# Feed-forward stage of a gated attention kernel: two chunks per turn on TensorE, weight splitting moved within the slot, two small buffers allocated first

## What is computed

```python
def block(x, w1, b1, w2, b2):            # the six feed-forward blocks, DIM 256, HIDDEN 1024
    h = gelu(einsum('bsd,hd->bsh', x, w1) + b1)
    return einsum('bsh,dh->bsd', h, w2) + b2 + x

xn = layernorm(x)
s = attention(xn, w_qkv, w_out)          # causal, 16 heads of 16
f = xn
for i in range(6):
    f = block(f, W1[i], B1[i], W2[i], B2[i])
    if i < 5:
        f = layernorm(f) * LN_G[i] + LN_B[i]
out = x + s * silu(f)
```

## Time and profile before

| | |
|---|---|
| median of three runs | 1671.97 us (1671.54 to 1676.83) |
| the profiled execution, its own time | 1672.36 us |
| its span in the trace | 1670.7 us |
| PE busy | 1617.1 us, 97% |
| PEld busy | 1314.5 us, 79% |
| DVE busy | 1169.8 us, 70% |
| ACT busy | 856.2 us, 51% |
| POOL busy | 317.8 us, 19% |
| mean granted clock of TensorE | 0.992 |

### The profile page before, as it was taken

The page is one execution under the profiler, slowest core; times in us unless marked ns, Lnnn a source line. Parts: engine busy times, 40 slices in busy tenths (PEclk is TensorE's granted clock), DMA queues, the critical chain, the costliest instruction groups (busy, mean ns, idle before and its releaser), DMA issues. The chain is left out here.

```text
span 1670.7 us, 28636 instructions
## 1 busy us (share of the span) xinstructions
PE 1617.1 (97%) x11024; PEld 1314.5 (79%) x11024; DVE 1169.8 (70%) x2932; ACT 856.2 (51%) x1164; POOL 317.8 (19%) x305
## 2 busy tenths in 40 slices
PE   6989999999999999999999999999999899999998
PEld 5879988889888888888888888888989844444443
DVE  7826777777777777777777677776565568787753
ACT  3444444444443444444444444444444499798986
POOL 1021111111111111111111111111011123343333
PEclk9989999999999999999999999999999989999999
DMA  8868724536002002012030020022020135565341
GB/s 276 320 173 209 174 62 109 116 73 140 15 7 61 8 16 49 7 34 42 7 51 8 23 51 9 14 39 80 1 71 1 45 114 163 162 187 178 117 116 58
DMA packets 76017, 141.46 MB, mean 85 GB/s; under 512 B 10172, under 2 KB 52924, under 8 KB 68540
## 3 DMA queue, kind: packets, MB, share of 16 engines
q1 hardware_dynamic: 75880, 139.62, 32.0%
HBM read 109.44 MB, written 55.31 MB: 99 GB/s over the span
## 5 line engine op out<-in xcount | busy, mean ns | idle before, releaser
L646 ACT ACTIVATE m_hid<-m_h_ps,m_b1s 128x512 f32<-128x512 f32 x384 | 265.3, 691 | 694.1 <-PE m_h_ps L749 674.6
L712 DVE TENSOR_TENSOR m_hidl<-m_hid,m_hidh 128x512 fp32r<-128x512 f32 x384 | 283.1, 737 | 266.5 <-ACT m_hidh L649 265.6
L993 ACT ACTIVATE a_prob<-a_st_ps 128x1024 f32<-128x1024 f32 x288 | 277.6, 1023 | 40.4 <-PE a_st_ps L1079 36.9
L762 PE MATMUL m_y_ps<-shared,m_hidh 128*128 128x256 f32 x1536 | 283.1, 282 | 0.0
L749 PE MATMUL m_h_ps<-m_xth,shared 128*128 128x512 f32 x768 | 275.7, 400 | 6.3 <-issue 3.9
L613 POOL TENSOR_TENSOR xres<-xres,m_b2s 128x1024 f32<-128x1024 f32 x48 | 132.1, 2753 | 744.1 <-DVE xres L665 744.1
L649 ACT ACTIVATE m_hidh<-m_h_ps,m_b1s 128x512 fp32r<-128x512 f32 x384 | 261.7, 682 | 0.0
L762 PEld LDWEIGHTS m_y_ps<-shared,m_hidh 128*128 128x128 f32 x1536 | 246.8, 188 | 14.5
L762 PE MATMUL m_y_ps<-w2h,m_hidh 128*128 128x256 f32 x768 | 216.9, 282 | 0.0
L762 PE MATMUL m_y_ps<-shared,m_hidl 128*128 128x256 f32 x768 | 215.3, 280 | 0.0
L762 PE MATMUL m_y_ps<-w2l,m_hidh 128*128 128x256 f32 x768 | 214.2, 279 | 0.0
(11 more groups left out here) (121 smaller groups left out, 2656.6 us busy)
## 6 DMA issues: line engine op xcount, KB each, us to landing
shared<-k_stacks SPq DMA_DIRECT2D x14, 896.0 KB
shared<-q_stacks SPq DMA_DIRECT2D x14, 896.0 KB
q_stacks<-q_parts SPq DMA_DIRECT2D x96, 128.0 KB
k_stacks<-k_parts SPq DMA_DIRECT2D x96, 128.0 KB
q_parts<-mq SPq DMA_DIRECT2D x16, 512.0 KB, 4.3
k_parts<-mk SPq DMA_DIRECT2D x16, 512.0 KB, 3.8
mk<-k_stacks SPq DMA_DIRECT2D x20, 384.0 KB, 10.7
raw<-w1t SPq DMA_DIRECT2D x48, 128.0 KB, 2.3
```

Of the source, the lines that this page charges most:

```text
L646: nc.scalar.activation(hid[n % 2][:], h_ps[n % 2][:], ACT.Gelu, bias=b1s[i % 2][:, k:k + 1])
L712: nc.vector.tensor_tensor(hidl[n % 4][:], hid[n % 2][:], hidh[n % 4][:].bitcast(F32), ALU.subtract).then_inc(low_done, 1)
L762: m = nc.tensor.matmul(y_ps[:, j, :], h[n % 4][:, j * P:(j + 1) * P], w[par][:, k, :], start=(k == 0 and j % 2 == 0 and h is hidh and w is ...
L993: nc.scalar.activation(to, scores, ACT.Exp).then_inc(exp_done, 1)
```

## The change

TensorE takes two chunks per turn: `up(n)`, `up(n + 1)`, the transposes where they are due, the visit of chunk `n`, `down(n - 2)`, `down(n - 1)`, the visit of chunk `n + 1`. The visits stand at `k` = 0, 1, 2, 4 and 5 of a slot in place of 1 to 6. On VectorE the steps of the epilogue move: `add_y` from `k = 0` to 1, the statistics from 2 to 4, aggregation and variance from 3 and 4 to 5, scaling from 5 to 6, the last step from 6 to 7. `split_piece` moves from `k = 7` to `k = 2`. The constants `mhalf` and the first maxima buffer `x_mx0` are made before all other buffers.

```diff
-        s.mx = [b.sb(f"x_mx{u}", [P, 2, HG, QT]) for u in range(2)]
+        s.mx = [*mx, b.sb("x_mx1", [P, 2, HG, QT])]
...
+        VISITED = (0, 1, 2, 4, 5)
         AT = {}
         for v in range(VISITS):
-            n = 6 * (SLOTS - FROM) * v // VISITS
-            AT.setdefault(CH * (FROM + n // 6) + 1 + n % 6, []).append(v)
+            n = len(VISITED) * (SLOTS - FROM) * v // VISITS
+            AT.setdefault(CH * (FROM + n // len(VISITED)) + VISITED[n % len(VISITED)], []).append(v)
...
-                if k == 0:
+                if k == 1:
                     add_y(t, 0)
                     add_y(t, 1)
...
-                if k == 2:
+                if k == 4:
                     dve.wait_ge(b2_added, t + 1)
...
-                elif k == 3:
+                elif k == 5:
                     dve.wait_ge(stats_done, t + 1)
...
-                elif k == 4:
                     dve.wait_ge(mean_done, t + 1)
...
-                elif k == 5:
+                elif k == 6:
...
-                elif k == 6:
+                elif k == 7:
...
-                if k == 7 and t < LAST:
+                if k == 2 and t < LAST:
                     dve.wait_ge(raw_loaded[g % 2], 32 * (t // 2 + 1))
                     split_piece(nc, dve, keep, (i + 1) % 2, g, w_high, t + 1).then_inc(w_split, 1)
...
-            for n in range(CHUNKS + 2):
+            for n in range(0, CHUNKS + 2, 2):
                 if n < CHUNKS:
                     up(n)
+                    up(n + 1)
                 if n % CH == 2 and n // CH + 1 < SLOTS:
                     turn(n // CH + 1)
+                for v in AT.get(n, ()):
+                    search.pe_visit(pe, s_ps, v, True)
                 if n >= 2:
                     down(n - 2)
-                for v in AT.get(n, ()):
+                    down(n - 1)
+                for v in AT.get(n + 1, ()):
                     search.pe_visit(pe, s_ps, v, True)
...
+        mhalf = b.sb("mhalf", [P, TILES])
+        mx = [b.sb("x_mx0", [P, 2, HG, QT])]
         apart = [b.sb(f"apart{u}", [P, PAIR * SEQ], F32R) for u in range(2)]
         shared = [b.sb(f"shared{n}", [P, HALVES * HID], F32R) for n in range(4)]
```

More of the change, by code:

```diff
@@ L135, with __init__ @@
 class MaxSearch:
-    def __init__(s, nc, b, scratch, keep):
+    def __init__(s, nc, b, scratch, keep, mx):
         s.nc, s.scratch = nc, scratch
@@ L721, in _ @@
                     search.dve_visit(dve, s_ps, v)
-            epilogue(SLOTS - 1, 0)
+            epilogue(SLOTS - 1, 1)
         @block.tensor
@@ L1152, in gated_block @@
         keep = {
-            "ident": b.sb("ident", [P, P]), "mhalf": b.sb("mhalf", [P, TILES]), "causal": b.sb("causal", [P, BANK]),
+            "ident": b.sb("ident", [P, P]), "mhalf": mhalf, "causal": b.sb("causal", [P, BANK]),
             "ones": b.sb("ones", [SPARE, 1, P]),
@@ L1167, in gated_block @@
         }
-        search = MaxSearch(nc, b, scratch, keep)
+        search = MaxSearch(nc, b, scratch, keep, mx)
         with ExitStack() as inner:
```

## The result

The changed kernel takes 1651.67 us (median of four runs, 1651.39 to 1652.38) against 1672.84 us for the kernel before in the same comparison: 0.987 of its time, with a 95% interval of 0.9852 to 0.9888. The profiled execution's span is 1650.7 us, 20.0 us less than before.

A forecast was written before the change was run, and what follows sets the result against it. TensorE's list was taken to bound stage two, 1236.5 of 1670.7 us. Terms -10.7 (block starts), -1.7 (clock), +15.7 (first split), -10 (visits), -9 (buffers) sum to -15.7 us: 1656.3 us forecast, range 1649 to 1668.

The forecast's parts named there:

- block starts: Five block starts where TensorE waits for the weight split: the split at `k = 2` removes the waits, -10.7 us.
- first split: Slot 0: VectorE waits for `raw` at the early split, TensorE stands 13.4 us before `down(3)`, then half clock; +15.7 us.
- visits: TensorE's nineteen stage-two waits for VectorE's maxima: 9 to 19 us, less 4 at most at `k = 5`; -10 us taken.
- buffers: First weight set moved to the second's addresses up to a multiple of 8192, to match its pace: -9 us, bounds 0 and 10.
- pairs as such: Grouping TensorE's list by two chunks: no gap at either seam between first and second products, so costed at nothing.
- in slot 1 and later `raw` is in time: Slot 1 onward: weight DMAs arrive before the early split needs them, all else being 15.7 us later too.
- rival 3: Visits at `k = 5`: VectorE's chain 0.6 us longer, so 42 visits lose 0.7 us each; 1695 us, slower; chance 0.06.
- The steps of the layer norm: Their moves within the slot on VectorE: result needed eight slots later, so hidden, at nothing.
- Rival 1: First weight set slow for its region or partner operands, so the address term is nothing: 1665.3 us; chance 0.25.
- Rival 2: Address term nothing and visits gain nothing, `k = 5` giving back the rest: 1672 us, no change; chance 0.1 with neighbours.
- Rival 4: Slot 0's pause does not come because the DMAs into `raw` land early: 1640.6 us; chance 0.04.
- slot 40 "nearly as early": Sign in the timeline: slot 3 starts some 15 us later than before, slot 40 nearly as early.

The follow-up runs named there:

- a2: The changed kernel with `mhalf` and `x_mx0` back in their old places: 1662.70 us, 0.9937 of the kernel before.
- b4: The changed kernel with TensorE's list back to one chunk per turn, all other edits kept: 1656.03 us, 0.9903 of the kernel before.
- a1: The changed kernel with the two DMAs of the first weight eighth ahead of the layout work in SyncE's list: 1643.63 us, 0.9826 of the kernel before.
- a7: The changed kernel with two weight pieces fetched ahead of the layout work and the third ahead of slot 1's search loads: 1637.16 us, 0.9789 of the kernel before.
- a3: The changed kernel with the split back at `k = 7`: 1661.17 us, 0.9928 of the kernel before.
- b2: The kernel before with only `split_piece` moved from `k = 7` to `k = 2`: 1687.77 us, 1.0087 of the kernel before.
- b1: The kernel before with only `mhalf` and `x_mx0` made first: 1666.38 us, 0.9957 of the kernel before.
- a4: The changed kernel with only `mhalf` made first, `x_mx0` not: 1653.78 us, 0.9887 of the kernel before.
- a6: a7 with 32 unused bytes per partition ahead of `raw`, the weights staying in place: 1659.44 us, 0.9909 of the kernel before.

## Why the prediction was right

I forecast 1656.3 us, in a range of 1649 to 1668, by a sum of -15.7 us. The time is 1651.67, 21.2 us below the run of before beside it and 20.0 us by the spans. The mechanisms came as told, one of them not where I had put it, and two terms were too small.

| term | forecast, us | measured, us | read from |
|---|---|---|---|
| block starts | -10.7 | -10.3 | 0.11 us at block 3 for 2.18, five times |
| clock at block 4 | -1.7 | -1.7 | no such stretch after |
| first split | +15.7 | +16.2 | slot 1's start, less slot 0's |
| visits | -10 | -11 | waits of 4.5 us gone, distances at the visits |
| buffers | -9 | -9.5 to -11 | a2 |
| pairs as such | 0 | -3.7 to -4.4 | b4 |

The visits' -11 is an estimate, good to some 2 us since a few per cent of the matmuls' rows are missing: the excess of the distances at visits over what a stream has is 13.4 us over the stage before and 5.8 after, of which 3.7 (41 x 0.09 us) is the seam behind transposes, which the kernel before has too, at a second product. The measured terms add up to -20.0 us with the smaller values and -22.2 with the larger, against -20.0 in the spans.

*The first split.* The chain was right step by step: VectorE's wait of 19.0 us (I said some 18), the last ready product at 114.9 (115.0), the subtraction at 128.04 and the pause of 13.6 (13.4), half clock behind it. a1 shows the cause, since with the DMAs early slot 1 starts at 122.41. The step "in slot 1 and later `raw` is in time" held only because the pause itself had given SyncE 16 us; in a1, without it, two later pieces were late. It takes three pieces (a7).

*The block starts.* Gone, as worked out. I did not see what a3 shows: with the layer norm's last step at `k = 7`, ahead of a split left there, the late split would have cost 24 us, so that in this kernel the edit is worth twice the 12 us that it is worth before.

*Visits.* The size was near, the reasoning was not. I counted on pairs giving the maximum both `down` to finish in. b4, without pairs, has no visit waits either; what helps is that visits and VectorE's heavy steps stand at other `k`. In the changed kernel no wait is left at the tight `k = 5`, so rival 3 did not come.

*The steps of the layer norm, "hidden, at nothing".* True of the changed kernel and wrong of the edit: b2 shows that with the steps in their old places the early split loses 12 us more than I had expected of it, and the kernel is slower than before; a3 shows that the last step would lengthen the gap at a late split. This cover was part of the change's gain, and I should have written what the split costs at a chunk that also holds the statistics.

*The grouping, "at nothing".* This is the term of the sum that was furthest off. b4 puts it at 4.4 us. I had looked at the seams, where there is no gap, and not at the first second products behind a seam, which follow each other 3 to 7 ns more slowly than the later ones. The distances account for 2.8 us of it.

*The buffers.* The bound from the earlier trace rows, 9.6 us, was right: a2 gives 9.5 us up to the last second product and 11.0 in the medians. Rival 1 has fallen. Of the two rules of the Trainium skill that I had weighed against this term, the first does not fit these runs. TensorE: Matmul & The Clock Gate, section "Wait — 56ns, not 53.3ns?", gives a distance by column count alone, and here, with the order of a7 and only buffers moved, 512 columns take 230 to 233.5 ns and 256 columns 114.5 to 119.2 ns. SBUF — State Buffer, section "Who interferes with whom", says that TensorE never waits on anyone, which can be so and still leave this, as the same work of the other engines runs beside both rates.

*Rival 2* (visits and addresses nothing) fell with a2. *Rival 4* did not come in the changed kernel, but its price was right to a few us: forecast 1640.6 for a kernel without the pause; a7, which takes the pause out, is 14.5 us below the changed one.

My sign of slot 40 "nearly as early" did not follow from my own sum, by which slot 40 had to be 15 us earlier or nearly so; it is 17.8 us earlier.

**Open.** Why the distance between the starts of two SBUF tiles should set TensorE's pace, and whether the distance modulo 256 or the places of the first set decide it (a first set that is 64 apart at other places would tell). Why second products just behind first ones are slower. b1's missing 4 us: 1.7 us of its profiled execution is the second stretch of half clock and 1.6 us lies at visits, but whether its other executions had that stretch is not known.

## What to carry to other kernels

Before an instruction that waits for a DMA is moved earlier in a hand-written list, read when that DMA is issued and what stands ahead of it in the issuing engine's list; here a few lines that moved three fetches ahead of the layout work gave nearly as much again (14.5 us) as the whole change (21.2 us). Where two tiles of the same kind run at different paces in one kernel, compare their addresses with those of their partner operands, and try a pad of 32 or 64 bytes: here 32 bytes ahead of the first set gained 9 us (a4 against a2), and 32 bytes ahead of `raw` cost 22 (a6 against a7). And an edit that is "hidden" should be tried without its companions on paper: the early split alone made this kernel slower. The other way round, what a moved step costs depends on what stands behind it: in a3 the norm's last step, moved ahead of the split, stands for 1.6 of the 3.1 us lost at a block start, by the timeline.

## What the runs showed of the hardware

TensorE's pace in these fp32r streams depends on where its operands start, by 2 to 3 ns in 230 (512 columns) and 3 to 4 ns in 115 (256 columns), as in the table above.

The granted clock can fall behind a gap of two to three us on TensorE, but does not always: it fell behind one of five gaps of 2.1 us before, behind two of the same five in b1, and behind four of five of 3.1 us in a3.

VectorE's cast of 128x256 elements, 0.28 us elsewhere, took 3.58 us at one place in a7, where it now runs beside GpSimd's memsets (timeline of a7):

```profile
107.71 3.55 POOL L610 MEMSET mq<- 128x2048 f32 x2 [36.83 <-DMA k_parts<-mk]
...
107.83 3.58 DVE L257 CAST w1h<-raw 128x256 fp32r<-128x256 f32 x1
...
131.51 0.28 DVE L257 CAST w1h<-raw 128x256 fp32r<-128x256 f32 x1
```

It cost nothing there, since TensorE was busy ahead of it; that the memsets are the cause was read from the times alone and not tried.
